# Order of stores, weight tests and later inputs in one DMA queue of a fused attention and feed-forward kernel

## The reference

```python
x = x + xattn(layernorm(x), ctx, ctx, ctx)       # gelu(x ctx^T) * (x ctx^T), times ctx; 120 context rows
u = layernorm(x)
h = silu(u @ w1.T * s1) * (u @ w2.T * s2)        # 256 -> 1024
h = gelu(h @ h1.T * t1)                          # 1024 -> 1024
h = gelu(h @ h2.T * t2)                          # 1024 -> 1024
x = x + h @ w3.T * s3                            # 1024 -> 256
```

## Time and profile before

| | |
|---|---|
| Runs | median 330.63 us of 3 (330.08 to 330.73) |
| Profiled execution, first to last instruction | 328.7 us; the 2.0 us between it and the median lie around the span or between executions |
| PE busy | 320.8 us (98%) |
| DVE busy | 263.9 us (80%) |
| ACT busy | 218.2 us (66%) |
| POOL busy | 41.7 us (13%) |
| HBM | 49.36 MB read, 6.29 MB written |
| Granted TensorE clock | full all through |

### The profile page before, as it was taken

The page is one execution under the profiler, slowest core; times in us unless marked ns, Lnnn a source line. Parts: engine busy times, 40 slices in busy tenths (PEclk is TensorE's granted clock), DMA queues, the critical chain, the costliest instruction groups (busy, mean ns, idle before and its releaser), DMA issues.

```text
span 328.7 us, 4727 instructions
## 1 busy us (share of the span) xinstructions
PE 320.8 (98%) x1628; PEld 271.5 (83%) x1628; DVE 263.9 (80%) x494; ACT 218.2 (66%) x367; POOL 41.7 (13%) x67
## 2 busy tenths in 40 slices
PE   7899999999999999999999999999999999999994
PEld 5799888788878888889998888888887888888994
DVE  4877996886995999997679475498899798987594
ACT  3567556574895876869835545977589687875840
POOL 5355010100000013003020002000000000100000
PEclk9999999999999999999999999999999999999999
DMA  6699999977738654755007033335575853443003
GB/s 205 243 282 284 206 272 325 417 262 277 234 139 296 215 193 128 208 182 177 11 2 255 3 128 128 131 127 194 214 241 183 296 217 128 128 136 122 0 30 107
DMA packets 23213, 60.22 MB, mean 183 GB/s; under 512 B 1680, under 2 KB 7568, under 8 KB 20624
## 3 DMA queue, kind: packets, MB, share of 16 engines
q0 software_dynamic: 13440, 37.75, 37.7%
q1 hardware_dynamic: 9744, 22.11, 19.9%
HBM read 49.36 MB, written 6.29 MB: 169 GB/s over the span
## 4 chain that ended last, share of the span: by engine, by line
PE 86%; DMA 6%; DVE 5%; issue 1%; POOL 1%; ACT 0%; DVEq 0%; POOLq 0%
PE P L1308 58%; PE P L1260 14%; PE P L1337 9%; DMA blocks_h<-H 3%; PE P L1224 2%; DMA WR<-blocks_h 2%; PE P L1216 2%; PE P L1232 1%; DVE TR L910 1%; DMA xs<-in_x 1%; DVE st L794 0%; DVE H L1039 0%; DVE H L1037 0%; DVE H L1035 0%; DVE H L1034 0%
## 5 line engine op out<-in xcount | busy, mean ns | idle before, releaser
L1308 PE MATMUL P<-TR,WR 128*128 128x512 f32 x896 | 206.0, 391 | 0.3 <-DMA WR<-blocks_h 0.3
L1308 PEld LDWEIGHTS P<-TR,WR 128*128 128x128 f32 x896 | 167.5, 188 | 36.6 <-DVE H L926 1.1
L603 ACT ACTIVATE TR<-H 128x512 fp32r<-128x512 f32 x112 | 68.1, 626 | 30.0 <-DVE H L905 27.3
L910 DVE TENSOR_TENSOR TR<-H,TR 128x512 fp32r<-128x512 f32 x112 | 73.8, 687 | 8.5 <-ACT TR L603 6.8
L1260 PE MATMUL P<-X,W 128*128 128x512 f32 (+1 forms) x320 | 62.5, 351 | 0.0
L1260 PEld LDWEIGHTS P<-X,W 128*128 128x128 f32 x320 | 51.7, 189 | 7.6
L905 DVE TENSOR_TENSOR H<-H 128x512 f32<-128x512 f32 x64 | 42.0, 685 | 0.0
L883 DVE SCALAR_TENSOR_TENSOR H<-P,sc,SLY 128x512 f32<-128x512 f32 (+1 forms) x40 | 25.2, 638 | 18.6 <-PE P L1260 10.0
L593 ACT ACTIVATE SLY<-P,sc 128x512 f32<-128x512 f32 (+1 forms) x40 | 23.9, 603 | 17.9 <-PE P L1260 15.3
L617 ACT ACTIVATE H<-P 128x512 f32<-128x512 f32 x48 | 27.8, 593 | 10.8 <-PE P L1308 10.8
L637 ACT ACTIVATE H<-H,sc 128x512 f32<-128x512 f32 x40 | 27.4, 715 | 10.7 <-DVE H L926 10.7
(11 more groups left out here) (74 smaller groups left out, 183.6 us busy)
## 6 DMA issues: line engine op xcount, KB each, us to landing
WR<-blocks_h POOLq DMA_DIRECT2D x16, 1024.0 KB, 4.8
WR<-in_h POOLq DMA_DIRECT2D x12, 1024.0 KB, 5.2
H<-in_h POOLq DMA_DIRECT2D x8, 512.0 KB, 16.1
blocks_h<-H SPq DMA_DIRECT2D x4, 1024.0 KB, 9.9
SLY<-in_h SPq DMA_DIRECT2D x8, 512.0 KB, 4.2
SLY<-in_w SPq DMA_DIRECT2D x6, 512.0 KB, 4.0
W<-in_w POOLq DMA_DIRECT2D x2, 1024.0 KB, 8.8
WR<-in_w POOLq DMA_DIRECT2D x2, 1024.0 KB, 5.2
```

Source lines behind the costliest of these rows:

```text
L603: eng.activation(TR[:, f % RING, 0, :], operand(c, L, s, kk), ACT.Copy).then_inc(s_hi, 1)
L910: eng.tensor_tensor(TR[:, f % RING, 1, :], operand(c, L, s, kk), TR[:, f % RING, 0, :].bitcast(f32), ALU.subtract).then_inc(s_lo, 1)
L1308: out_ = eng.matmul(bank(c, L, s, m)[:, :], WR[r % WRING][:, at:at + 128], TR[:, f % RING, h, :], start=(s in FRESH[L] and kk == 0 and h = ...
```

## The change

The four `sums_out` go directly behind each other, right behind `load_cf(1)` and `load_ct(1)`. `load_check(0)` and `load_check(1)` follow. Only then come batches 4 to 7, contexts 2 and 3 and s3. In the first chunk tests 0 and 1 stand beside product (0, 0, 6) instead of tests 1 and 2; test 0 is gone from product (0, 0, 2); tests 2, 3 and 4 stand where 3, 4 and 5 stood; and test 5 stands beside product (0, 1, 3), where none was. Tests 6 to 21 stay.

```diff
         TESTS = 22
-        BESIDE = {(0, 0, 2): (0,), (0, 0, 6): (1, 2), (0, 1, 0): (3,), (0, 1, 1): (4,), (0, 1, 2): (5,),
+        BESIDE = {(0, 0, 6): (0, 1), (0, 1, 0): (2,), (0, 1, 1): (3,), (0, 1, 2): (4,), (0, 1, 3): (5,),
                   (0, 1, 4): (6,), (0, 1, 5): (7,), (0, 1, 6): (8,)}
...
             load_cf(1)
             load_ct(1)
+            for p in range(4):
+                sums_out(p)
+            load_check(0)
+            load_check(1)
             load_x(4)
             load_x(5)
             load_cf(2)
             load_ct(2)
-            sums_out(0)
             load_x(6)
             load_x(7)
-            sums_out(1)
             load_cf(3)
             load_ct(3)
-            sums_out(2)
-            sums_out(3)
             eng.dma_start(s3b[:, :], s3.broadcast_to([128, D])).then_inc(s_s3, 16)
-            for i in range(9):
+            for i in range(2, 9):
                 load_check(i)
```

## The result

The changed kernel takes 329.46 us (median of 8 runs, 329.28 to 329.89), the kernel before 330.41 (8 runs, 329.98 to 330.77) beside it. The ratio is 0.9973, 95% interval 0.9963 to 0.9983: 0.95 us or 0.27% faster. The forecast was 329.6, with "faster by over 0.2%" at 0.66.

What follows compares the result with a forecast made beforehand. PE was taken as the bound, so only its waits could be won: 0.45 us at the first product plus 0.55 at product (0, 0, 6), 1.0 us off 330.63, gives 329.6 us. The range was 329.1 to 330.5.

Steps and rivals of the forecast that it cites:

- What PE loses: Twelve products of chunk 0 against the equal twelve of chunk 1: chunk 0 loses 1.03 us that chunk 1 does not.
- The wait for WR: At the first product, 63.75: PE waits for weights loaded behind store 1; an earlier store gains 0.45 us.
- the relief of the raw loads: Batches 4, 5 and context 2 gone from 16 to 27 us: raw loads end earlier; counted at nothing.
- the 2.8 us: In SP's queue: batches 6 and 7, between stores 0 and 1, delay store 1 by 2.8 us; it lands at 54.2 without them.
- the shared rate: While two queues share the engines, q1, which carries the stores and inputs, gets 0.19 MB a us.
- my 4.4 us: Store 1, 1 MB: about 2.0 us plus bytes at 436 GB/s makes 4.4 us, against 10.23 in the trace.
- DVE's lateness: At product (0, 0, 6): moving test 0 starts DVE's totals near 86.5 instead of 89.83; gain 0.55 us.
- the price of 330.1 us for a cured wait for WR alone: Rival: only one of the two gains comes, at the first product or at product (0, 0, 6); 330.1 us, chance 0.20.
- Test 5 and the lengthened row of DVE: Beside product (0, 1, 3): test 5 adds 1.22 us on DVE, 1.1 us are left to spare; priced at nothing.
- The inputs behind the tests' data: Inputs moved to about 68 may disturb POOL's weight load for product (0, 0, 4); bound 0 to 0.5 us, taken as 0.
- The slower rival: Test 5's tile late on ACT, DVE 5.1 us later, product (0, 1, 4) waits 2.1 us: 331.7 us, chance 0.06.

Runs made afterwards that it cites:

- the kernel with only the early inputs moved: Kernel before with batches 4 and 5 and context 2 moved behind the loads of tests 0 and 1, tests in the new places: 329.45 us, ratio 0.9987.
- the kernel with context 3 ahead: Kernel before with the two loads of context 3 (0.5 MB) moved ahead of store 1, all else as before: 329.93 us, ratio 0.9994.
- the queue alone: Kernel before with only SP's queue order changed, tests in their old places: 329.58 us, ratio 0.9988; a second time 329.77 us, ratio 0.9991.
- the tests alone: Kernel before with only the places of tests 0 to 5 changed, old queue order: 330.14 us, ratio 1.0001; a second time 329.98 us, ratio 0.9995.
- The added work: Changed kernel with four unused DVE subtractions (2.4 us) behind test 5, beside product (0, 1, 3): 331.06 us, ratio 1.0036 to the kernel before.
- The kernel with the tests' data last: Kernel before with the four stores first, then the inputs, then the tests' loads; test 0 stays beside product (0, 0, 2): 337.38 us, ratio 1.0225.

## Why the prediction was right, and where it wasn't

**What PE loses.** Right. Two equal stretches of the same kernel, set against each other, gave 1.03 us; the trace after has 1.05 less and the times 0.95. That the size came out so well is partly luck. The loss varies, and the profile that I read has the slowest raw load of all fourteen (29.7 us). The second profile of the kernel before lost 0.64 us, and the second pair of times differs by 0.52 us.

**The wait for WR, 0.45 us.** Right in size (the first product starts at 63.30 instead of 63.75), because layer1(1) caps it. The term behind it was mis-sized: I let store 1 land 2.8 us earlier, at 54.2, and in the profile after it landed 4.7 us earlier (5.5 us instead of 10.23); over all profiles it is 4.2 us. The middle inputs account for 2.9 us of that. What I left out was the relief of the raw loads, "I count nothing for it". The slowest raw load took 21.5 us after, against 29.7, and the kernel with only the early inputs moved shows that this half alone suffices. That the 2.8 us are the bytes of the middle inputs at the shared rate isn't shown, since moving them shortened the raw loads as well. And the same rate, carried on without end, misled me in the kernel with context 3 ahead: 0.2 us more of waiting where I had said 2.1 to 2.7. The fit behind my 4.4 us is given in the Trainium skill ("DMA: Bandwidth & Descriptors", section "Anatomy of one DMA") for the path of DMAs that POOL issues. For store 1, which SP issues, the profiles have 10.23 us, 5.5 us in the profile after, and 4.2 us in the second profile of the queue alone, where the last raw load had landed at 28.5 + 19.5 = 48.0. So the estimate is close where little else is in the way.

By the Trainium skill ("DMA: Bandwidth & Descriptors", section "Queues, rings and completion order") each engine goes round-robin between the queues that have work, packet by packet. The trace agrees: 490 and 482 packets in the earlier trace rows. A likely reason why either half of the move helps follows from it: what leaves the one queue shortens the time in which both have work. That is an inference; no run here varies it by itself.

**DVE's lateness, 0.55 us.** Right in place, nearly right in size: totals at 86.60 where 86.5 was forecast, an idle time for PE before the second four, one idle time of the weight loads left. The term measured 0.47 to 0.48 us: the tests alone took the 384 matmuls from 87.97 to 87.50, and 0.12 us of the 0.58 belonged to WR. Wrong in what it hangs on. I gave this term to the move of test 0 alone and added the two terms as if each stood by itself. The queue alone does it too, since test 0's data comes in time, and the row of latenesses above shows that the terms aren't separate: with DVE as late as ever, an earlier PE waits longer by what it won. The step that failed is the addition, and with it the price of 330.1 us for a cured wait for WR alone: without a cure for DVE it would, by that row, have won almost nothing. The sum held because the change does both.

**Test 5 and the lengthened row of DVE.** Right. 1.1 us were forecast to be left at product (0, 1, 5). In the profile after, the first low part is done at 134.20 + 0.69 = 134.9, and PE comes to it at 63.46 + 10 x 7.27 = 136.2 at the latest, so 1.1 to 1.3 us. The added work agrees with it.

**The inputs behind the tests' data.** Right that they cost nothing: no wait of PE for WR or for batch 4 is in the trace. The kernel with the tests' data last shows how near the other order is to a loss of 8 us. The slower rival named this mechanism for test 5 and priced it at 2.1 us; for test 0 it is real, and larger than I priced it, since ACT's queue holds more than the one instruction I followed.

## What to carry to other kernels

Compare two stretches of equal work in one profile: the difference is what the waits cost, and it is a better bound than any list of waits. Before adding up two repairs, ask whether the second is late against the clock or against the engine that the first sets free. And of a load that an engine waits for in its own order, price all that is queued behind the waiting instruction, the copies that free a bank among them.

## What the runs showed of the hardware

- After PE had waited 4.95 us, the granted clock was 0.50, that is 1.2 of 2.4 GHz, for 3.1 us, and matmuls of 512 columns started 0.427 us apart. In the profile before, with no wait of more than 1.0 us behind the first matmul, it stayed full. By these numbers the stall cost about 1.4 us more than itself. It is one execution with one such stall; what a shorter one would cost isn't shown.
- One kernel's DMAs end at different times from execution to execution: the slowest raw load of the kernel before took 29.7 us in one profile and 25.3 in another. The wait of 0.45 us for WR was there in the first and not in the second.
- The same store of 1 MB took 10.23 us where the raw loads ran beside it until 57.8, 5.5 us where they ended at 28.1 + 21.5 = 49.6 (the profile after), and 4.2 us where they ended at 48.0 (the second profile of the queue alone).
